# Three small moves in a written-out order of work: two jobs of the units 4n+2, the turning of the second batch's x, and a piece of context

## The chip, the cores and the metric

The kernel runs on one core of one Trainium2 chip. Its time is the device time of one execution in microseconds (us); lower is better. A profiled execution gives, for each engine, when each instruction ran. The engines are TensorE (PE, with its weight loads PEld), VectorE (DVE), ScalarE (ACT), GpSimd (POOL) and SyncE (SP), which here only issues transfers.

## The reference, cut to what matters

```python
B, LQ, D, LK = 4, 256, 512, 1601        # 32 query heads, 8 key heads of 128
q = layernorm(x) @ Wq + bq
k, v = split(ctx @ Wkv + bkv)
o = softmax(q @ k.T / sqrt(128)) @ v     # per batch and head; 4 query heads share k, v
x = x + tanh(g_xattn) * (o @ Wo + bo)
y = layernorm(x)
x = x + tanh(g_ffn) * (y @ base_W.T + top-2-of-8 LoRA experts of y)
```

All in float32. The matrix products of the attention are done as three products of rounded parts (high x high, high x low, low x high).

## The kernel before, in words

The attention is cut into 64 **units** U (4 batches of NU = 16), each with two query heads of one batch, 256 queries each, so 512 columns. A unit has 13 **slots** t, one for each tile of 128 context rows (the last has 65). Slot s = 13 U + t. In each slot PE does, first, three matmuls of scores into one of two psS buffers (L641), then three of probabilities x values for the tile of 19 slots before (L656 to L658), and then the **jobs** that a table gives to the slot (L663). The same table sets the order of work of all the other engines: each goes through the slots and waits on semaphores.

What follows a score tile: ACT copies it to xs (L917, called at L1018), DVE takes the running maximum into mrun (L1335), POOL subtracts the maximum (L846), ACT takes the exponential twice, as f32 (L1044) and rounded into ph (L1047), and DVE makes the low part pl (L1105) and the running sum psum_ (L1368). POOL does these two for one tile of a unit in the first batch, for three tiles in the others (L850, L855, L861). Scores of slot s may not start before the copy and the maximum of slot s - 2 are done (L638 to L640).

The jobs, by letter, with the unit n that they serve: m and s turn the running maximum and sum (n = U - 1, U - 2), b spreads the maximum over the lanes, q0 and q1 are the projections of the next unit's queries, k0 to k3 four pieces of Keys (k3 is 450 columns wide, the others 384), v0 to v12 pieces of Values, o0 and o1 the halves of the output projection of U - 2, p0 and p1 the same of U - 3, x0 and x1 turn the next batch's normalized x, r spreads the reciprocal sums by PE (in most units a transfer through memory does that instead, L984 to L995, and r is passed over; PE does it for the units n with n % 16 in (0, 12), so in the slots of U % 16 in (2, 14)).

The table has a row for each U % 4: AT in the first units, AT_MEM from U = 4 on, and TURN for the units 18, 34 and 50. The units 6, 10, 14, 22, 26, 30, 38, 42, 46, 54, 58 and 62 thus take the third row of AT_MEM, the row that the change edits.

Each job takes one of four banks of PSUM psW (`take`, L421). `free` is a queue in the order of issue: a job gets the bank that has been in the queue longest and waits for whoever empties it (`emptied`, L428): o and p halves are emptied by DVE's add into acc (L1144), k by DVE's kl (L1116), q by ql (L1128), s and m by reductions on DVE (L1266, L1244), b and r by ACT. From slot 6 on two banks hold attention outputs (pv), so two are left for the jobs.

The weights and the next batches' context are cut into high and low parts by POOL during the first batch (`cuts`, L837 and L839): the raw piece is fetched by SP to one of four staging buffers (`fetches`), and the parts go on to memory. The 16 pieces (c, n) of the second batch's context share one buffer cst, so each waits until the one before has been stored; x of the next batch is loaded to xraw and cst after the last of them (L774 to L778), normalized by POOL in slot 8 of unit 14, 30 or 46 (L896 to L900), and turned by PE in slots 11 and 12 of that unit.

In the loop of DVE, slot 26 (unit 2, t = 0) ends with the inverse standard deviation of six row tiles (L1393 to L1396).

Of the kernel before, what the change touches and what calls it, by code (L numbers as in the profile page):

```python
# [18 lines left out]
def gated_block(nc: bass.Bass, x, ctxT, gx, gf, wq, bq, wk, wv, bkv, wo, bo, bw, rw, la, lb,  # L19
# [12 lines left out]
    NU = 16  # L32
    UN = B * NU
# [16 lines left out]
    def lead(U):  # L50

        return 1 if U < NU else 3
# [3 lines left out]
    MEM_LO, MEM_SUM = 2, UN - 3  # L56

    def sum_by_mem(U):
        return MEM_LO <= U < MEM_SUM and U % NU not in (0, NU - 4)
# [9 lines left out]
    def on_slot(V):  # L69

        return 9 if sum_by_mem(V) else 8 if V < UN - 2 else 10 if V == UN - 2 else 6
# [3 lines left out]
    AT = [  # L75
# [4 lines left out]
    ]  # L80
    AT_MEM = [
# [4 lines left out]
    ]  # L86

    TURN = "m,v11 p0 b,v12 k2 p1 s k3 r q0 - q1 - o0"
    for U in range(UN + 2):

        names_of = {0: "k1 - k2 v0 q0 k3 q1 v1 - v2 - v3 -", UN: "- - - - - - - - s r - - o0",
                    UN + 1: "- p1 - - s c o0 o1",
                    UN - 1: "m - b - p1 s - r - - o0 - -"}.get(U, TURN if U > NU and U % NU == 2 else (AT_MEM if U >= MEM_LO + 2 else AT)[U % 4])
        for t, names in enumerate(names_of.split()):
            for name in names.split(","):
                kind, part = name[0], int(name[1:] or 0)
                n = {"m": U - 1, "b": U - 1, "s": U - 2, "r": U - 2, "o": U - 2, "p": U - 3, "q": U + 1, "v": U // 4,
                     "c": U - 2, "k": (U + 1) // 2, "x": U // NU + 1, "-": -1}[kind]
                top = {"m": UN, "b": UN, "s": UN, "r": UN, "o": UN, "c": UN, "p": UN - 1, "q": UN, "v": 4 * B, "k": NK, "x": B, "-": 0}[kind]
                if not 0 <= n < top or (kind == "x" and U % NU < 14):  # L100
                    continue
                if kind == "r" and sum_by_mem(n):
                    continue
                jobs[NT * U + t].append(("o" if kind == "p" else kind, n, part))
# [9 lines left out]
    def halves(kind, n):  # L114
        return [(kind, n, a) for a in range(2 if kind in "vo" else 1)]
# [7 lines left out]
    for U in range(NU + 1):  # L123
        at, u = NT * U, U % 4
        if U + 2 < NU:
            cuts[at + (9 if u == 2 else 7)] += halves("q", 2 * U + 4)
            cuts[at + (11 if u == 2 else 9 if u % 2 else 8)] += halves("q", 2 * U + 5)
        if u % 2 == 0 and U // 2 + 1 < 8:
            cuts[at + (8 if u == 2 else 9)] += halves("k", U // 2 + 1)
        if u == 3 and U // 4 + 1 < 4:  # L130
            for a in range(2):
                cuts[at + 9 + a].append(("v", U // 4 + 1, a))
        if U != 1:
            for a in range(2):
                cuts[at + (12 if U == 0 else 13 if u in (0, 3) else 18) + a].append(("o", max(U - 1, 0), a))
        for t in (9, 11) if u == 1 else (11,) if u != 3 or U == 3 else ():
            if spare:
                cuts[at + t].append(spare.pop(0))
    for n in range(16, 16 * (B - 1)):
        b, i = divmod(n, 16)  # L140
# [6 lines left out]
    stage, there, s = [], [[] for _ in range(4)], 0  # L147
    for no, (p, at) in enumerate(cut_at):
# [5 lines left out]
        if no >= len(first) + 2:  # L154
            s = max(s, at - 10, cut_at[last][1] + 1)
# [7 lines left out]
    with ExitStack() as ctx:  # L163
        def sb(name, shape, dt, c=ctx):
            return c.enter_context(nc.sbuf_tensor(name, shape, dt))
# [64 lines left out]
        x1 = sb("x1", [128, NQ - 2, 512], F32)  # L230
# [157 lines left out]
        for T in range(TN):  # L388
            U, t = divmod(T, NT)
# [705 lines left out]
        def _(eng):  # L1095
# [218 lines left out]
            def goes_first(kind, n, part):  # L1314

                return kind == "s" and sum_by_mem(n)

            def goes_later(kind, n, part):

                return kind == "yl" or kind == "o" and n == UN - 2  # L1320
# [16 lines left out]
            for s in range(SLOTS):  # L1337
                U, t = divmod(s, NT)
                b, u = divmod(U, NU)
                V = U - 2  # L1340
                for j in jobs.get(s - 1, []):
                    if goes_first(*j):
                        after_job(*j)
                if sum_by_mem(V):
                    divide(V, t - on_slot(V))
                if s < TN - 1:
                    running_max(s)
                if s == TN - 2:
                    running_max(TN - 1)
                    add_o(UN - 3, 0)  # L1350
                    row_max(UN - 1)
                if 0 <= V < UN and not sum_by_mem(V):
                    divide(V, t - on_slot(V))
                for j in jobs.get(s - 1, []):
                    if (j[0] not in "ms" or not TN - NT < s <= TN) and not goes_first(*j) and not goes_later(*j):
                        after_job(*j)
                T = s - EXP
                if 0 <= T < TN and T % NT >= lead(T // NT):
                    UT, tt = divmod(T, NT)
                    rows = rows_of(tt)  # L1360
                    p, total = exp_place(T), psum_[0:rows, UT % 2, :]
                    dve.wait_ge(s_h, T + 1)
                    lower(pl[0:rows, T % RP, :], p, ph[0:rows, T % RP, :]).then_inc(s_l)
                    if tt > lead(UT):
                        dve.wait_ge(s_a, a_count[T] - 1)
                    else:
                        dve.wait_ge(s_lp, lp_count[NT * UT])
                    eng.tensor_tensor(total, p, total, ALU.add).then_inc(s_a)  # L1368
                    if T == TN - 1:
                        total = psum_[:, UT % 2, :]  # L1370
                        dve.wait_ge(s_a, a_count[T])
                        dve.wait_ge(s_ap, 2 * (UT - NU) + 1)
                        eng.tensor_tensor(total, pair_of(UT)[:, 0, :], total, ALU.add).then_inc(s_a)
                for j in jobs.get(s - 2, []):
                    if goes_later(*j):
                        after_job(*j)
                if TN - NT <= s < TN:
                    for j in jobs[s]:
                        if j[0] in "ms" and not goes_first(*j) and j[1] != UN - 1:
                            after_job(*j)  # L1380
                if s in (0, 2):
                    lower_ctx(2 + s // 2)
                if s in (4, 13, 21):
                    r = (4, 13, 21).index(s) + 1
                    dve.wait_ge(s_acc, 16 * r)
                    for i in range(2):
                        stats(2 * r + i, acc[:, i, :])
                if s == 23:
                    floored_var(2, NQ)
                if s == 27:  # L1390
                    dve.wait_ge(s_bvh, 1)
                    lower(bvl[:, :], bkv_sb[:, 15:16], bvh[:, :]).then_inc(s_bvl)
                if s == 26:  # L1393
                    inverse_dev(2, 2, NQ)
                    eng.tensor_scalar(rstds[:, 2:NQ], rstd[:, 2:NQ], SCALE, None, ALU.mult).then_inc(s_stat)
                    dve.wait_ge(s_stat, 1)  # L1396
                if u == 2 and t == 6 and 1 <= b < B:
                    for i in range(2):
                        dve.wait_ge(s_acd, 32 * b)
                        stats(2 * b - 2 + i, acc[:, i, :])  # L1400
                if s == NT * (UN - 7) - 2:
                    floored_var(0, NQ - 2)
                if s == NT * (UN - 7):
                    inverse_dev(3, 0, NQ - 2)
                for i in {TN - 18: (0,), TN - 17: (1,), TN - 12: (3,), TN - 10: (5,)}.get(s, ()):
                    ffn_norm(i)
                if s == TN - 5:
                    dve.wait_ge(s_rtb, 1)
                    route_off(1)
                if s == TN - 3:  # L1410
                    route_first(1)
                if s == TN + 3:
                    route_second(1)
                if s == TN + 4:
                    route_weights(1)
# [84 lines left out]
```

## Time and profile before

| | |
|---|---|
| median of 3 runs | 2310.38 us (2306.56 to 2311.54) |
| the profiled execution's own time | 2311.37 us |
| its span | 2309.3 us |
| mean granted TensorE clock | 0.996 of full |
| instructions | 37402 |

The span is the time from the first to the last instruction of the profiled execution; its own time has some 2 us more. An engine's busy time is the time in which it ran instructions, and idle time is put down to the engine and line that it waited for.

### The profile page before, as it was taken

How to read it: one execution, taken by the hardware profiler on the slowest of the kernel's cores; microseconds unless marked ns; L12 is line 12 of the kernel's file. 1: busy time of each engine (PE TensorE's matmuls, PEld its weight loads, DVE VectorE, ACT ScalarE, POOL GpSimd, SP SyncE). 2: the span in 40 equal slices, each digit the busy share in tenths (PEclk: the TensorE clock that was granted, in tenths of full speed). 3: DMA queues.
4: the chain of work that ended last, by engine and by line, in shares of the span. 5: the costliest groups of instructions: out<-in, count | busy, mean ns of one | idle time of the engine just before them, and what ended most of it. 6: DMA issues, size and time to landing. Idle time of an engine off the chain costs nothing.

```text
span 2309.3 us, 37402 instructions
## 1 busy us (share of the span) xinstructions
PE 2262.2 (98%) x12363; PEld 1941.8 (84%) x12363; DVE 1815.1 (79%) x3167; ACT 1666.7 (72%) x3152; POOL 1633.0 (71%) x1372
## 2 busy tenths in 40 slices
PE   7999999999999999999999999999999999999998
PEld 6888888887888888888888888888888888888865
DVE  5888888887887787787778787787787778787786
ACT  4777777776777777777777777777777777777772
POOL 4888786977568678757658678776767756766772
PEclk9999999999999999999999999999999999999999
DMA  7344353564233242326213333333422213222111
GB/s 258 121 167 133 111 173 100 173 199 162 87 111 111 94 160 94 133 79 209 92 43 137 116 128 116 111 127 118 157 86 96 92 60 110 66 98 90 66 68 55
DMA packets 137567, 271.85 MB, mean 118 GB/s; under 512 B 21664, under 2 KB 54944, under 8 KB 137120
## 3 DMA queue, kind: packets, MB, share of 16 engines
q1 hardware_dynamic: 122400, 255.71, 32.6%
q10 hardware_dynamic: 14976, 13.74, 2.6%
q8 instruction: 101, 1.65, 0.3%
q14 instruction: 90, 0.74, 0.1%
HBM read 202.44 MB, written 66.97 MB: 117 GB/s over the span
## 4 chain that ended last, share of the span: by engine, by line
PE 79%; DVE 9%; POOL 5%; issue 3%; ACT 3%; DMA 1%; ACTq 0%; SPq 0%; POOLq 0%; DVEq 0%
PE psW L432 12%; PE psW L434 11%; PE psW L433 11%; PE psS L432 7%; PE psS L434 7%; PE psS L433 7%; PE psW L656 6%; PE psW L657 6%; PE psW L658 6%; POOL xs L846 3%; PE psW L488 3%; DVE psum_ L1368 3%; DVE mrun L1335 2%; PE psW L496 1%; DVE pl L1105 1%
## 5 line engine op out<-in xcount | busy, mean ns | idle before, releaser
L846 POOL TENSOR_TENSOR xs<-xs,mb 128x512 f32<-128x512 f32 (+1 forms) x832 | 1068.9, 1310 | 472.3 <-ACT mb L917 472.3
L1335 DVE TENSOR_TENSOR mrun<-psS,mrun 128x512 f32<-128x512 f32 (+1 forms) x704 | 482.8, 686 | 340.1 <-ACT xs L917 337.5
L917 ACT ACTIVATE xs<-psS 128x512 f32<-128x512 f32 (+1 forms) x832 | 496.0, 596 | 245.1 <-PE psS L434 232.4
L1105 DVE TENSOR_TENSOR pl<-psP,ph 128x512 fp32r<-128x512 f32 (+1 forms) x672 | 459.8, 684 | 81.5 <-ACT ph L1047 76.2
L1047 ACT ACTIVATE ph<-xs 128x512 fp32r<-128x512 f32 (+1 forms) x832 | 518.9, 624 | 3.3 <-PE psW L658 3.1
L1368 DVE TENSOR_TENSOR psum_<-psP,psum_ 128x512 f32<-128x512 f32 (+1 forms) x672 | 457.4, 681 | 1.0 <-POOL pl L850 0.9
L1044 ACT ACTIVATE psP<-xs 128x512 f32<-128x512 f32 (+1 forms) x672 | 401.2, 597 | 29.4 <-DVE rinv L1268 12.9
L432 PE MATMUL psS<-ql,kh 128*128 128x512 f32 (+1 forms) x832 | 340.3, 409 | 6.3 <-DVE mrun L1335 5.2
L656 PE MATMUL psW<-ph,vh 128*128 128x512 f32 (+1 forms) x832 | 335.4, 403 | 3.6 <-POOL pl L850 3.3
L433 PE MATMUL psS<-qh,kh 128*128 128x512 f32 (+1 forms) x832 | 328.8, 395 | 0.0
L434 PE MATMUL psS<-qh,kl 128*128 128x512 f32 (+1 forms) x832 | 328.7, 395 | 0.0
L657 PE MATMUL psW<-pl,vh 128*128 128x512 f32 (+1 forms) x832 | 328.3, 395 | 0.0
L658 PE MATMUL psW<-ph,vl 128*128 128x512 f32 (+1 forms) x832 | 328.2, 394 | 0.0
L432 PE MATMUL psW<-wvl,ch 128*128 128x256 f32 (+1 forms) x832 | 238.9, 287 | 0.0
L434 PE MATMUL psW<-wvh,cl 128*128 128x256 f32 (+1 forms) x832 | 233.9, 281 | 0.0
L433 PE MATMUL psW<-wvh,ch 128*128 128x256 f32 (+1 forms) x832 | 233.0, 280 | 0.0
L656 PEld LDWEIGHTS psW<-ph,vh 128*128 128x128 f32 (+1 forms) x832 | 156.5, 188 | 49.5 <-issue 7.2
L657 PEld LDWEIGHTS psW<-pl,vh 128*128 128x128 f32 (+1 forms) x832 | 157.2, 189 | 38.0 <-issue 2.4
L658 PEld LDWEIGHTS psW<-ph,vl 128*128 128x128 f32 (+1 forms) x832 | 156.6, 188 | 38.3
L434 PEld LDWEIGHTS psS<-qh,kl 128*128 128x128 f32 (+1 forms) x832 | 153.3, 184 | 39.4
L432 PE MATMUL psW<-cl,wkh 128*128 128x384 f32 (+1 forms) x512 | 178.8, 349 | 5.2 <-DVE cl L1105 5.2
L434 PE MATMUL psW<-ch,wkl 128*128 128x384 f32 (+1 forms) x512 | 178.9, 349 | 0.0
(208 smaller groups left out, 4382.8 us busy)
## 6 DMA issues: line engine op xcount, KB each, us to landing
wqh<-scr_wq SPq DMA_DIRECT2D x96, 256.0 KB, 2.6
wql<-scr_wq SPq DMA_DIRECT2D x96, 256.0 KB, 3.0
woh<-scr_wo SPq DMA_DIRECT2D x48, 512.0 KB, 3.3
wol<-scr_wo SPq DMA_DIRECT2D x48, 512.0 KB, 4.2
rbc<-scr_r ACTq DMA_DIRECT2D x52, 256.0 KB, 3.4
scr_wq<-wqh SPq DMA_DIRECT2D x32, 256.0 KB, 2.1
scr_wq<-wql SPq DMA_DIRECT2D x32, 256.0 KB, 2.5
scr_wo<-woh SPq DMA_DIRECT2D x16, 512.0 KB, 2.6
```

Source lines behind the costliest of these rows:

```text
L432: eng.matmul(o, lh, rl, start=first, stop=False)
L433: eng.matmul(o, lh, rh, start=False, stop=False)
L434: return eng.matmul(o, ll, rh, start=False, stop=last)
L656: eng.matmul(o, vh[0:rows, t, hs], hi, start=t == 0, stop=False)
L657: eng.matmul(o, vh[0:rows, t, hs], lo, start=False, stop=False)
L658: eng.matmul(o, vl[0:rows, t, hs], hi, start=False, stop=t == NT - 1).then_inc(s_pv)
L846: eng.tensor_tensor(tile, tile, mb[0:rows_of(t), U % 2, :], ALU.subtract).then_inc(s_sub)
L917: return eng.activation(hi, src, ACT.Copy)
L1047: eng.activation(ph[0:rows, T % RP, :], xs[0:rows, T % RX, :], ACT.Exp).then_inc(s_h)
L1105: return eng.tensor_tensor(lo, src, f32(hi), ALU.subtract)
L1335: eng.tensor_tensor(run, psS[0:rows, s % 2, :], a, ALU.max).then_inc(s_m)
L1368: eng.tensor_tensor(total, p, total, ALU.add).then_inc(s_a)
```

## The change

Five edits, all of order.

1. In the third row of AT_MEM, p0 goes from slot 4 to slot 1, k3 from slot 6 to slot 4, and in slot 7 the order of r and p1 is swapped.
2. For the second batch, x0 and x1 go from slots 11 and 12 of unit 14 to slots 1 and 2 of unit 15, where q0 goes from slot 1 to slot 7 (NEXT_X). Load and normalization of x stay where they are, and so do the turns of the third and fourth batch.
3. POOL cuts the context piece c3 in slot 26 instead of 37, and c4 in slot 37 instead of 50 (`(9, 11, 13) if U == 1`, and no `or U == 3`). Slot 50 loses its piece. The fetches move with them.
4. DVE's inverse standard deviation goes from slot 26 to slot 30 (unit 2, t = 4).
5. The condition on x names the three units.

```diff
@@ AT_MEM @@
-        "m,v11 - b,v12 k2 p0 s k3 r,p1 q0 - q1 x0 o0,x1",
+        "m,v11 p0 b,v12 k2 k3 s - p1,r q0 - q1 x0 o0,x1",
...
+    NEXT_X = "m x0 b,x1 k0 p1 s k1 q0 q1 k2 - o0 o1"
...
-                    UN - 1: "m - b - p1 s - r - - o0 - -"}.get(U, TURN if U > NU and U % NU == 2 else (AT_MEM if U >= MEM_LO + 2 else AT)[U % 4])
+                    NU - 1: NEXT_X, UN - 1: "m - b - p1 s - r - - o0 - -"}.get(U, TURN if U > NU and U % NU == 2 else (AT_MEM if U >= MEM_LO + 2 else AT)[U % 4])
...
-                if not 0 <= n < top or (kind == "x" and U % NU < 14):
+                if not 0 <= n < top or (kind == "x" and U not in (NU - 1, 2 * NU - 2, 3 * NU - 2)):
...
-        for t in (9, 11) if u == 1 else (11,) if u != 3 or U == 3 else ():
+        for t in (9, 11, 13) if U == 1 else (9, 11) if u == 1 else (11,) if u != 3 else ():
             if spare:
                 cuts[at + t].append(spare.pop(0))
...
-                if s == 26:
+                if s == 30:
                     inverse_dev(2, 2, NQ)
```

## Rows read from the trace of the kernel before

**Rows 1.** The page, busy us (share of the span) and instructions of each engine.

```profile
PE 2262.2 (98%) x12363; PEld 1941.8 (84%) x12363; DVE 1815.1 (79%) x3167; ACT 1666.7 (72%) x3152; POOL 1633.0 (71%) x1372
```

**Rows 2.** PE's waits: engine, line, waited for: us in total, times, longest.

```profile
PE psS L432 <- DVE mrun L1335: 5.2, 9, 0.7
...
PE psW L432 <- DVE kl L1116: 4.0, 5, 0.9
PE psW L656 <- POOL pl L850: 3.3, 3, 1.6
PE psW L488 <- POOL xraw L900: 2.8, 1, 2.8
```

**Rows 3.** Timeline, slots 11 and 12 of unit 14: start, us, instruction, [idle before].

```profile
537.02 0.39 PE L432 MATMUL psS<-ql,kh 128*128 128x512 f32 x1
...
541.41 0.65 PE L488 MATMUL psW<-ident,xraw 128*128 128x128 f32 x4 [2.83 <-POOL xraw L900]
...
546.62 0.48 PE L432 MATMUL psS<-ql,kh 128*128 128x512 f32 x1
```

**Rows 4.** A stretch of windows: busy of each engine, clock, DMA share, GB/s.

```profile
541.40:545.00 3.60, 3.59 (x12) 2.83 (x13) 1.27 (x3) 2.23 (x4) 3.60 (x3) 0.60 1.01 362
```

**Rows 5.** Timeline of POOL in unit 14, slots 8 to 12.

```profile
530.25 0.62 POOL L837 TENSOR_SCALAR woh<-pp 128x512 fp32r<-128x512 f32 x1 [7.93 <-PE psW L434]
...
541.34 2.08 POOL L900 TENSOR_SCALAR cst<-cst,mv,rstds 128x512 f32<-128x512 f32 x1
```

**Rows 6.** Timeline of PE in unit 30, from slot 7 to the start of unit 31.

```profile
1082.55 0.40 PE L432 MATMUL psS<-ql,kh 128*128 128x512 f32 x1
...
1086.90 0.39 PE L432 MATMUL psS<-ql,kh 128*128 128x512 f32 x1
...
1088.30 0.28 PE L432 MATMUL psW<-xtl,wqh 128*128 128x256 f32 x1
...
1093.93 0.39 PE L432 MATMUL psS<-ql,kh 128*128 128x512 f32 x1
...
1098.89 0.48 PE L432 MATMUL psS<-ql,kh 128*128 128x512 f32 x1
```

**Rows 7.** Timeline of DVE in unit 30, slot 8.

```profile
1088.43 0.69 DVE L1335 TENSOR_TENSOR mrun<-psS,mrun 128x512 f32<-128x512 f32 x1 [1.88 <-ACT xs L917]
...
1089.63 0.74 DVE L1144 SCALAR_TENSOR_TENSOR acc<-psW,tg,acc 128x512 f32<-128x512 f32 x1
```

**Rows 8.** Timeline of PE in unit 22: scores of slots 6 to 10 and 12.

```profile
803.45 0.47 PE L432 MATMUL psS<-ql,kh 128*128 128x512 f32 x1
807.39 0.40 PE L432 MATMUL psS<-ql,kh 128*128 128x512 f32 x1
810.15 0.39 PE L432 MATMUL psS<-ql,kh 128*128 128x512 f32 x1
812.97 0.39 PE L432 MATMUL psS<-ql,kh 128*128 128x512 f32 x1
814.36 0.40 PE L432 MATMUL psS<-ql,kh 128*128 128x512 f32 x1
...
819.31 0.42 PE L432 MATMUL psS<-ql,kh 128*65 128x512 f32 x1 [0.58 <-DVE mrun L1335]
```

**Rows 9.** Timeline of DVE in unit 22, slots 6 and 9.

```profile
805.18 0.18 DVE L1268 RECIPROCAL rinv<-ssum 128x4 f32<-128x4 f32 x1
...
814.13 0.69 DVE L1308 TENSOR_TENSOR psW<-psW,rbc 128x512 f32<-128x512 f32 x1
```

**Rows 10.** Timeline of DVE in unit 2, slots 1 and 5.

```profile
93.09 1.22 DVE L1162 TENSOR_TENSOR steps<-steps 128x6 f32<-128x6 f32 x1
...
107.15 0.69 DVE L1335 TENSOR_TENSOR mrun<-psS,mrun 128x512 f32<-128x512 f32 x1 [2.73 <-ACT xs L917]
```

**Rows 11.** Timeline of PE in unit 2, slot 2, and in unit 4, slot 6.

```profile
96.30 0.65 PE L496 MATMUL psW<-ident,nm 128*128 128x128 f32 x4 [1.21 <-DVE nm L1244]
...
172.81 0.47 PE L656 MATMUL psW<-ph,vh 128*128 128x512 f32 x1 [1.59 <-POOL pl L850]
```

## The prediction

> **What bounds the kernel now.** I read the page first: PE is busy for 2262.2 us, 98% of the span, the next engine for 79% [rows 1]. So time can only be won where PE stands still, 47 us in all, and the change adds and removes no matmul. Then PE's waits, which say for whom it stands [rows 2]: nine times for the running maximum (L1335, 0.7 at most), five times for a bank that kl empties (4.0 us), three times for POOL's pl (3.3), once for the normalized x (2.8). Then the timelines around those waits, and last the starts of the score matmuls, one for each slot, since the length of a slot shows a stall that is split over several instructions. In unit 22 a slot with no job takes 1.39 us (812.97 to 814.36), one with an output half 2.76 (slot 7), one with k3 3.94 (slot 6) [rows 8]. k3 so costs 3.94 - 1.39 = 2.55 (some 0.1 of it the slot's start behind a turn), a half 1.37. A move shifts PE's work, and what matters is how far DVE, ACT and POOL are behind PE afterwards.
>
> **Edit 2, x turned later.** In unit 14 PE stands 2.83 us before the first turn, for POOL's normalization [rows 3], and its clock then reads 0.60 over 3.6 us [rows 4], that is, most of them at 1.2 GHz. POOL is late because it stood 7.93 us for p1 in slot 7 and then worked without a break to 543.4 [rows 5]. Slots 11 and 12 together take 546.62 - 537.02 = 9.60 us [rows 3]; the same slots with the same jobs in unit 30 take 1098.89 - 1093.93 = 4.96 [rows 6]. The stall costs 4.64 us, its clock included. After the change the first turn is due some three slots later, at least 4.96 + 1.7 us after 537.0, and the normalized tiles are there at 541.4 and 543.4, so the whole 4.64 goes. The two turns cost the same in unit 15. There q0 comes in slot 7 where the slot had no job; DVE so gets a longer slot 7 and is less behind. For the small stalls of that unit that this closes I take an estimate of 0.5, within 0 to 1. Lower bound of the gain: the stall comes back at another place because POOL still has its 18 us to do; the places it could stop are the exponentials of the first slots of unit 15, which need POOL's subtraction: 1 us given back. Sum for this edit -5.1, from -3.6 to -5.6.
>
> **Edit 4, the inverse.** In unit 2 DVE's six small instructions run from 92.03 to 94.9, 2.9 us, ahead of the maximum and of the reduction for b, and PE waits 1.21 us for that [rows 11]; q0 in the next slot waits another 0.5 for DVE's kl, in the same backlog. At the new place, after the work of slot 30, DVE stood idle for 2.73 us waiting for a score copy [rows 10]. 2.9 in 2.73 leaves 0.2 to go through to r, which already waited. Sum -1.5, from 0 to -1.9. One instruction there took 1.22 us for six columns [rows 10], where the reciprocal of four columns took 0.18 [rows 9], so the 2.9 hold some 1.7 us that are not arithmetic. The Trainium skill (GPSIMD Engine Reference, section Specifications) says that GpSimd shares its SBUF interface with VectorE and contends with VectorE instructions that have two SBUF inputs. The trace agrees: 1.22 us is the time of a product of two SBUF tiles while POOL was at work. By the rule the 2.9 us stay 2.9 at the new place, where POOL is at work too; without it they could be some 1.2, and the 0.2 would be 0.
>
> **Edit 3, the context piece.** Before slot 6 of unit 4 PE waits 1.59 us for POOL's pl [rows 11], at the end of 40 us in which POOL never stood. The piece of slot 50 lies in that stretch and its two instructions took 0.52 and 1.02 us, so 1.5 us of the 1.59 go. In slot 26 the piece costs the same, but there POOL stands 3.4 us for unit 1's maximum; the bias additions of slot 28 are pushed to where that wait ends. SP waits at its fetch of c4 until c3 is stored, up to the end of unit 2's slot 3; behind it in the queue lie only fetches that are due ten slots later. If POOL is late there, the exponentials of unit 2 wait: at most 1.5 us. Sum -1.5, from 0 to -1.6.
>
> **Edit 1 in eight units without r (6, 10, 22, 26, 38, 42, 54, 58).** Here PE stands before slot 12 for the maximum of slot 10, 0.58 us in unit 22 [rows 8], and that is the last link of DVE's chain. I followed unit 22 with the clock at the start of slot 6 (803.45). Before: rinv at 1.73 [rows 9], slot 9 at 9.52, the first step of dividing (L1308) at 10.68 [rows 9], slot 12 at 15.86 [rows 8]. From the division to slot 12 it is 5.18 us, and that stays: division, oh and two exponentials on ACT, pl, sum, ol, maximum. After: slot 6 has no job. PE gets to slot 7 at 1.5, slot 8 at 4.25, slot 9 at 7.07: 2.45 us earlier than before. DVE and ACT cannot follow by so much. The sum's reduction, rinv and the copy that ACT issues behind it hold ACT till 3.4; from there, copy of slot 7, two exponentials, and then six DVE instructions of 0.6 us (pl, sum, maximum, the addition of p1, pl, sum) put the division at about 8.8, 1.9 us earlier. So slot 12 starts at 8.8 + 5.2 = 14.0, where PE alone would be there at 12.7: the wait grows from 0.75 us (slot length 2.14 against 1.39) to 1.3. A small wait in slot 2 goes (0.1), since p0 is between m and b. Per unit +0.4, six units +2.6. In units 6 and 10 DVE has two more pairs of pl and sum at just this place (the first batch), so +1.7 each; but PE's later arrival gives POOL the time for which the units behind, 7 and 11, wait at slot 6 (two of the three waits for pl in [rows 2]), and I take +0.4 for both. Sum +3.0; from -6 (all the waits of 0.75 us gone, 8 x 0.75) to +6 (nothing given back in units 7 and 11, and 0.4 more in each).
>
> **Edit 1 in four units with r (14, 30, 46, 62).** Now the slot 7 of unit 30 takes 4.35 us (1082.55 to 1086.90) [rows 6], against 1.39 + 1.37 + 0.35 for r = 3.11: a stall of 1.24, p1 waiting for the bank that kl of k3 empties (0.88 of it shown, four of the five waits in [rows 2]). It goes: k3 is two slots earlier. But the order of banks moves with it. With two banks from slot 6 on, the banks go s, p1, r, q0: before, q0 took the one of r, which ACT empties at once. Now p1 comes before r, and q0 takes p1's bank, which is free only after DVE's addition of p1. DVE does that behind the maximum of slot 8, and that needs slot 8's scores copied. In unit 30 the addition starts at 1089.63 and takes 0.74, so it ends 3.47 us behind the start of slot 8 [rows 6, 7], and that chain starts from PE itself, so it keeps its length. q0 started 1.40 behind it [rows 6]. The new stall is 3.55 - 1.45 = 2.1 us. Behind it DVE has caught up. Net +0.9 less the 0.1 in slot 2: +0.8 in three units. In unit 14 DVE has the first batch's two more pairs, the wait is 2.5 and the net +1.2. Sum +3.6, from +2 to +5. Behind q0 wait slot 9's scores only; SP's loads of the next q weights follow q0 by 2 us and have two slots to spare.
>
> **Sum.** -5.1 - 1.5 - 1.5 + 3.0 + 3.6 = -1.5 us. The clock comes on top. After 2.83 us of standing it fell, and cost some 1.6 of the 4.64 (slot 12 of unit 14, 4.80 us, against 3.2 in unit 30). After the 1.59 us in unit 4 it stayed. The four new waits of 2.1 to 2.5 us lie between; I take one fall of four, +1.6, and for the range none to four. That makes +0.1 on the profiled execution's own 2311.4 us, so 2311.5; that execution lies 1.0 above the median of three. Against the median 2310.4 it gives 2310.5, and as the unfollowed small waits around unit 15 and unit 2 are more likely to close than to open, I say 2310.
>
> **Rivals.**
> A. The waits before slot 12 close instead of growing, because k3's and the half's DVE work is gone from slots 7 and 8. For it: kl at slot 7 and its 0.6 us are in the chain now. Against it: PE gains 2.45 us on that chain and the chain 1.9. It gives -1.5 - 3.0 - 6 = -10.5 us, 2300. Chance 0.13.
> B. Clock falls. The place is q0 in slot 8 of units 14, 30, 46 and 62; the price 1.6 us a piece; it decides if a standstill of 2.1 us is enough. With four falls -1.5 + 6.4 = +4.9, 2315.3; with the upper ends of edit 1 beside it, 2320. Slower by over 0.2%. Chance 0.17.
> C. The turn's stall is only moved: POOL's queue of 18 us shows in unit 15. Then 3.6 to 4.6 us less are won, -1.5 + 4.6 = +3.1 at most, 2313. Chance 0.1; two slots of margin speak against it.
> D. q0's wait doesn't appear, as DVE reaches the addition sooner than from the copy of slot 8. Against it: the order in the loop is written out, the maximum first. The new stalls (3.6) are then missing and the old ones (4 x 1.24) gone: -1.5 - 3.6 - 5.0 = -10.1, 2300. Chance 0.08.
> My forecast, gains and losses that cancel within 4 us: 0.52.
>
> Faster or slower by over 0.2% (4.6 us) is about what a measurement of this kernel can tell from no change. Faster: A, D and the lower tail of the forecast (0.06), 0.27. Slower: B's greater part (0.12) and a fifth of C: 0.14. Within: 0.59. Range 2301 to 2317: it holds A's near half and B with part of its upper ends.
>
> **What the profile would show.** Unit 14's slots 11 and 12 under 5 us together, no 1.2 GHz there. A PE wait of 2.1 us at the first wqh matmul of slot 8 in units 14, 30, 46, 62, on DVE acc L1144, in place of that on kl. Slot 11 of unit 22 at 2.7 us against 2.14. No wait for nm in unit 2, none above 0.2 for pl in unit 4. The prediction is wrong if slot 11 in unit 22 shrinks towards 1.4, or if slot 8 in unit 30 stays at 2.8.

## The result: slower by 0.5%

The changed kernel takes 2319.84 us in the median of 4 runs (2319.41 to 2320.86), the kernel before 2308.47 us in the runs beside it (2305.9 to 2311.54). The ratio is 1.0050, 95% interval 1.0038 to 1.0062. The forecast was 2310 and its range ended at 2317. The measured time lies above both: the kernel got slower where no change was expected. The profiled execution's own time is 2320.86 us, its span 2319.0, which is 9.7 more than before. (Lines of the changed kernel stand two higher: L1335 is now L1337.)

**After, the page.** The head of the page, and the busy time of each engine.

```profile
span 2319.0 us, 37387 instructions
...
PE 2267.6 (98%) x12363; PEld 1943.9 (84%) x12363; DVE 1817.6 (78%) x3167; ACT 1667.0 (72%) x3152; POOL 1630.4 (70%) x1372
```

Beside [rows 1] no engine has more work worth the name. PE's 5.4 us are the same matmuls, some of them at the lower clock.

**After, PE's waits.** Who ended them; us in total, times, longest.

```profile
PE psS L434 <- DVE mrun L1337: 10.3, 9, 2.6
...
PE psW L434 <- DVE acc L1146: 8.5, 4, 2.4
```

Beside [rows 2] the waits for kl (4.0) and for the normalized x (2.8) are gone from the head of the list, and no wait for POOL's pl is left in it. In their place stand 8.5 us on acc, four times, which the forecast had (8.8), and 5.1 more on the running maximum, one of them 2.6 long, which it had not.

**After, timeline of PE**, where the new stops and the starts of slots lie: unit 2 slot 7; unit 6 slots 11 and 12; unit 14 slots 8 and 11 and the start of unit 15; unit 22 slots 11 and 12; unit 30 slot 8.

```profile
107.11 0.47 PE L434 MATMUL psS<-ql,kh 128*128 128x512 f32 x1 [2.63 <-DVE mrun L1337]
...
258.78 0.50 PE L658 MATMUL psW<-ph,vh 128*128 128x512 f32 x1 [0.61 <-DVE pl L1107]
260.72 0.41 PE L434 MATMUL psS<-ql,kh 128*65 128x512 f32 x1 [0.98 <-DVE mrun L1337]
...
536.12 0.35 PE L434 MATMUL psW<-xtl,wqh 128*128 128x256 f32 x1 [2.37 <-DVE acc L1146]
...
541.83 0.39 PE L434 MATMUL psS<-ql,kh 128*128 128x512 f32 x1
...
545.99 0.39 PE L434 MATMUL psS<-ql,kh 128*128 128x512 f32 x1
...
816.91 0.39 PE L434 MATMUL psS<-ql,kh 128*128 128x512 f32 x1
819.32 0.42 PE L434 MATMUL psS<-ql,kh 128*65 128x512 f32 x1 [0.85 <-DVE mrun L1337]
...
1089.82 0.35 PE L434 MATMUL psW<-xtl,wqh 128*128 128x256 f32 x1 [2.06 <-DVE acc L1146]
```

Read against [rows 3], slots 11 and 12 of unit 14 take 545.99 - 541.83 = 4.16 us where they took 9.60: edit 2 does what it should. Read against [rows 8], slot 11 of unit 22 takes 2.41 where it took 2.14.

**After, timeline of DVE in unit 2**, the inverse in its new slot 30:

```profile
99.77 0.18 DVE L1162 RECIPROCAL rstd<-steps 128x6 f32<-128x6 f32 x1
99.98 1.29 DVE L1163 TENSOR_TENSOR steps<-rstd 128x6 f32<-128x6 f32 x1
101.30 1.22 DVE L1164 TENSOR_TENSOR steps<-steps 128x6 f32<-128x6 f32 x1
102.56 1.22 DVE L1165 TENSOR_SCALAR steps<-steps 128x6 f32<-128x6 f32 x1
103.82 1.20 DVE L1166 TENSOR_TENSOR rstd<-rstd,steps 128x6 f32<-128x6 f32 x1
105.05 1.20 DVE L1397 TENSOR_SCALAR rstds<-rstd 128x6 f32<-128x6 f32 x1
106.28 0.69 DVE L1337 TENSOR_TENSOR mrun<-psS,mrun 128x512 f32<-128x512 f32 x1
```

**After, timeline of POOL** over the same time:

```profile
97.44 2.54 POOL L848 TENSOR_TENSOR xs<-xs,mb 128x512 f32<-128x512 f32 x2
99.94 1.31 POOL L852 TENSOR_TENSOR pl<-psum_,ph 128x512 fp32r<-128x512 f32 x1
101.21 6.23 POOL L848 TENSOR_TENSOR xs<-xs,mb 128x512 f32<-128x512 f32 x5
```

The six instructions take 6.5 us, not 2.9, and then the maximum runs for which PE stands. Five of them work on six columns and take 1.2 us each; the reciprocal, on as many columns, takes 0.18. POOL starts an instruction at 101.21 and then about every 1.25 us (102.46, 103.70, 104.95, 106.17). The five DVE instructions end at 101.27, 102.53, 103.78, 105.01 and 106.24, each 0.06 to 0.08 us behind one of these starts. So it is one DVE instruction for each POOL instruction.

**After, clock in two stretches.** PE busy with its count, the granted clock, DMA share, GB/s:

```profile
108.00:114.50 6.50, 6.05 (x18) 0.50 0.54 184
...
1090.90:1094.30 3.40, 3.40 (x12) 0.51 0.34 91
```

Both are at 1.2 GHz, right behind a standstill (2.63 and 2.06 us).

**Where the 9.7 us are**, by the starts of the units' first slots, after less before: unit 2 +3.3; unit 4 -1.6; units 6 to 12 +4.2; unit 14 -4.1 and unit 15 +0.3; units 22, 26, 38, 42, 54, 58 +3.7; units 30, 46, 62 +5.9; unit 63 +0.8; all others together some -0.4; and -2.4 up to the end of unit 0, which no edit touches. There the profile before happens to have 1.2 GHz (granted clock 0.50) from 23.3 to 26.7 and from 30.2 to 37.0 us, where that of the changed kernel reads 1.00. The four other profiles of this study with two such stretches are within 0.2 us of the kernel before; the nine with less or none of it are 2.0 to 3.3 us shorter. So two single profiles can differ by 2 or 3 us where no edit is at work, and the units have to be compared one by one.

### The profile page after: what moved, and what is told of

Same layout as the page of the kernel before. It is cut to its first block, busy times and chain, and to the rows that moved or that the text cites. A ratio compares the mean times of both kernels' runs of the same rounds, so it can differ in the third digit from the quotient of the medians.

```text
span 2319.0 us, 37387 instructions
## 1 busy us (share of the span) xinstructions
PE 2267.6 (98%) x12363; PEld 1943.9 (84%) x12363; DVE 1817.6 (78%) x3167; ACT 1667.0 (72%) x3152; POOL 1630.4 (70%) x1372
## 4 chain that ended last, share of the span: by engine, by line
PE 83%; DVE 8%; issue 3%; ACT 3%; POOL 1%; DMA 1%; ACTq 0%; SPq 0%; DVEq 0%
PE psW L434 12%; PE psW L436 12%; PE psW L435 12%; PE psS L434 7%; PE psS L436 7%; PE psS L435 7%; PE psW L658 7%; PE psW L660 7%; PE psW L659 7%; PE psW L490 3%; DVE psum_ L1370 2%; DVE mrun L1337 2%; PE psW L498 1%; ACT ph L1049 1%; DVE pl L1107 1%
## 5 line engine op out<-in xcount | busy, mean ns | idle before, releaser
L1337 DVE TENSOR_TENSOR mrun<-psS,mrun 128x512 f32<-128x512 f32 (+1 forms) x704 | 481.9, 684 | 347.4 <-ACT xs L919 346.4
L434 PEld LDWEIGHTS psS<-ql,kh 128*128 128x128 f32 (+1 forms) x832 | 154.9, 186 | 28.5 <-ACT xs L919 11.3
```

The source lines that it names most:

```text
L434: eng.matmul(o, lh, rl, start=first, stop=False)
L1337: eng.tensor_tensor(run, psS[0:rows, s % 2, :], a, ALU.max).then_inc(s_m)
```

## The experiments

All are timed beside the kernel before, which took 2307.3 to 2309.0 us in the four sets. An expectation stands ahead of each result as it was put down before the run.

**1. The inverse back.** The changed kernel with edit 4 undone.

```diff
-                if s == 30:
+                if s == 26:
```

> The changed kernel with DVE's inverse deviation back in slot 26; all other edits stay. Theory P (port): at slot 30 five of its small instructions take 1.2 to 1.3 us each beside POOL's subtractions (0.8 and 1.2 us for two of them at slot 26), which stops PE for 2.6 us before slot 7 of unit 2 and then lowers its clock; so unit 2 gives back 4.5 to 5.5 us and the kernel is 2315 us. Rival C (the context piece): the wait in unit 2 comes from POOL being later by the piece in slot 26; then unit 2 still stands 2 to 3 us in slot 6 or 7 and the time is 2319 or 2320.

2317.23 us (2313.38 to 2318.25), 1.0036 (1.0024 to 1.0047). Unit 2 is 2.18 us shorter than before, and the stop before slot 7 is gone. Timeline of DVE, and below it of POOL, at the old place:

```profile
89.11 0.18 DVE L1162 RECIPROCAL rstd<-steps 128x6 f32<-128x6 f32 x1
89.33 0.17 DVE L1163 TENSOR_TENSOR steps<-rstd 128x6 f32<-128x6 f32 x1
...
90.13 0.17 DVE L1397 TENSOR_SCALAR rstds<-rstd 128x6 f32<-128x6 f32 x1
```

```profile
87.41 1.31 POOL L848 TENSOR_TENSOR xs<-xs,mb 65x512 f32<-65x512 f32 x1
90.64 0.51 POOL L839 TENSOR_SCALAR cst<-stg 128x384 fp32r<-128x384 f32 x1 [1.92 <-DMA scr_c<-pp]
```

POOL stands from 88.7 to 90.64 and each DVE instruction takes 0.17. So edit 4 costs 5.4 us of unit 2 in the profile, as expected. The time fell by 2.6 us between the medians (3.2 between the ratios, whose intervals allow 5.4), to 2317 and not to 2315; the spans of the two profiles differ by 3.6, since small waits and stretches at 1.2 GHz lie at other places too. Rival C is out. Further, the waits of slots 2 and 3 that edit 4 was to win go without it: with the context piece of edit 3 in slot 26, POOL stands for a store there, and the inverse runs in that pause.

**2. The inverse alone.** The kernel before with edit 4.

```diff
-                if s == 26:
+                if s == 30:
```

> The kernel before with the inverse deviation in slot 30 and nothing else. Theory P: unit 2 is longer by 3 to 5 us (a stop of about 2.6 us before slot 7, the clock at 1.2 GHz behind it, less the 1.2 + 0.5 us of waits in slots 2 and 3 that go): 2311 to 2313 us. Rival C: without the piece in slot 26 the stop is not there and the kernel is 1.5 to 2 us faster than before, 2307.

2311.75 us (2308.77 to 2313.61), 1.0013 (1.0004 to 1.0021). Unit 2 is 3.24 us longer: slots 2 and 3 give 2.19, slots 6 to 8 take 5.74. The five small instructions take 1.19 to 1.23 us here too. No context piece was moved, so it is not the piece: the stop before slot 7 (2.53 us) comes with the inverse alone.

**3. r ahead of p1.** The changed kernel with the old order in slot 7.

```diff
-        "m,v11 p0 b,v12 k2 k3 s - p1,r q0 - q1 x0 o0,x1",
+        "m,v11 p0 b,v12 k2 k3 s - r,p1 q0 - q1 x0 o0,x1",
```

> The changed kernel with the old order r, p1 in slot 7 of the row; k3 and p0 stay in slots 4 and 1. Theory B (banks): q0 in slot 8 of units 14, 30, 46 and 62 gets the bank of r, which ACT empties, in place of p1's, so the four stops of 2.0 to 2.4 us on the addition go, with the clock falls behind two of them: 10 to 12 us less in those slots. Something may come back in slots 9 to 12 as PE runs ahead of DVE: up to 1 us a unit. 2309 to 2312 us. Rival: the stop is DVE's backlog and not the bank; then PE stops as long in slot 9 or 10 and the time stays within 2 us of 2320.

2319.49 us (2314.02 to 2322.26), 1.0044 (1.0032 to 1.0057). The four stops at q0 are gone, and units 30 and 46 are each 0.9 us shorter than before: the bank was the reason. But the expected 2309 to 2312 was missed, and the number is the rival's. In this profile four other places are worse than in that of the changed kernel: unit 0 by 2.6 us (the two stretches at 1.2 GHz again), slot 6 of unit 2 by 5.2, slot 2 of unit 15 by 2.1, slot 10 of unit 62 by 2.4. The profiled execution, 2321.88 us, is among the slowest of six that spread over 8 us, so it is not shown that the others lost at the same places. Timeline of DVE in unit 2 and in unit 62:

```profile
102.50 8.31 DVE L1163 TENSOR_TENSOR steps<-rstd 128x6 f32<-128x6 f32 x1
...
2201.39 4.09 DVE L1181 TENSOR_SCALAR hn<-x,mv,rstd 128x512 f32<-128x512 f32 x1
```

A product of six columns took 8.31 us, over eight instructions that POOL ran in a row (101.5 to 110.8). It waits for POOL as the five of the changed kernel do, but for several instructions at a time.

**4. The later x and the context pieces alone.** The kernel before with edits 2, 3 and 5.

```diff
+    NEXT_X = "m x0 b,x1 k0 p1 s k1 q0 q1 k2 - o0 o1"
...
-        for t in (9, 11) if u == 1 else (11,) if u != 3 or U == 3 else ():
+        for t in (9, 11, 13) if U == 1 else (9, 11) if u == 1 else (11,) if u != 3 else ():
```

> The kernel before with the two edits that only moved waits of POOL: x turned in unit 15, and c3 and c4 cut earlier; the row and the inverse as before. By the unit lengths of the changed kernel: units 14 and 15 are 5 us shorter, unit 4 1.6 us shorter, nothing lost elsewhere: 2302 us, 0.3 % faster. Rival: the gains of unit 14 depend on the row's edit (k3 earlier), and only 2 to 3 us are won: 2305 us.

2303.53 us (2299.09 to 2304.76), 0.9975 (0.9966 to 0.9984): these two pay. Unit 2 -2.2, unit 4 -1.5, unit 14 -5.4, but unit 15 +2.4, so the later x alone wins 3.0 us in the two units and not the 5 that were expected. Timeline of PE in unit 15, slots 2 and 3, and of POOL ahead of it:

```profile
540.68 0.48 PE L434 MATMUL psS<-ql,kh 128*128 128x512 f32 x1
...
542.61 0.50 PE L658 MATMUL psW<-ph,vh 128*128 128x512 f32 x1 [0.98 <-DVE pl L1107]
...
544.40 0.65 PE L498 MATMUL psW<-ident,nm 128*128 128x128 f32 x4 [0.82 <-DVE nm L1246]
...
545.25 0.48 PE L434 MATMUL psS<-ql,kh 128*128 128x512 f32 x1
```

```profile
526.18 0.62 POOL L839 TENSOR_SCALAR woh<-pp 128x512 fp32r<-128x512 f32 x1 [7.92 <-PE psW L436]
...
535.21 2.11 POOL L902 TENSOR_SCALAR xraw<-xraw,mv,rstds 128x512 f32<-128x512 f32 x1
537.28 2.10 POOL L902 TENSOR_SCALAR cst<-cst,mv,rstds 128x512 f32<-128x512 f32 x1
539.32 5.05 POOL L848 TENSOR_TENSOR xs<-xs,mb 128x512 f32<-128x512 f32 x4
```

This is rival C at half its price: POOL's two normalizations stand ahead of the subtractions that unit 15 needs. In the changed kernel it hardly shows (slots 2 and 3 of unit 15 +1.0), since the stop at q0 in slot 8 of unit 14 has already made PE late; in experiment 3, without that stop, slot 2 of unit 15 takes 4.53 us as it does here (4.56), against 2.47 in the changed kernel.

**5. The row alone.** The kernel before with edit 1.

```diff
-        "m,v11 - b,v12 k2 p0 s k3 r,p1 q0 - q1 x0 o0,x1",
+        "m,v11 p0 b,v12 k2 k3 s - p1,r q0 - q1 x0 o0,x1",
```

> The kernel before with the new row of slots alone (edit 1: k3, p0, p1 and the output half in their new slots), all else as before. Theory R (the row is what costs, by three mechanisms that the profile after shows: the wait of q0 in slot 8 of the four units with r for the bank of p1, 2.0 to 2.4 us each; a wait before slot 12 of the other eight units that is some 0.4 us longer each; and a clock fall here and there behind them): units 30, 46, 62 together +4 to +6 us, the six units from 22 on together +3.7, units 6 to 12 +4, so 2317 to 2319 against a before of 2308.5. Rival (the row itself cost near nothing, and what unit 30 and the others lose comes with the later x or the inverse): 2308 to 2311.

2321.15 us (2317.81 to 2324.7), 1.0059 (1.0045 to 1.0072), more than the 2317 to 2319 that I had put on it. The rival is out. By units: 6 to 12 +4.8; 22, 26, 38, 42, 54, 58 +4.4; 30, 46, 62 +5.9; 14 -1.7; 63 +0.9. Its waits of PE:

```profile
PE psW L432 <- DVE acc L1144: 8.5, 4, 2.4
PE psS L432 <- DVE mrun L1335: 7.9, 8, 1.0
...
PE psW L656 <- DVE pl L1105: 3.7, 9, 0.6
```

The factors of experiments 5, 4 and 2 multiply to the result: 1.0059 x 0.9975 x 1.0013 = 1.0047, against 1.0050 measured. So, within the intervals, the row is all of the loss; the others nearly cancel, to -0.12%.

**6. The good half of the row.** The kernel before with a row of its own in units 14, 30, 46 and 62.

```diff
+    TURN_R = "m,v11 p0 b,v12 k2 k3 s - r,p1 q0 - q1 x0 o0,x1"
...
-                    UN - 1: "m - b - p1 s - r - - o0 - -"}.get(U, TURN if U > NU and U % NU == 2 else (AT_MEM if U >= MEM_LO + 2 else AT)[U % 4])
+                    UN - 1: "m - b - p1 s - r - - o0 - -"}.get(U, TURN_R if U > 4 and U % NU == 14 else TURN if U > NU and U % NU == 2 else (AT_MEM if U >= MEM_LO + 2 else AT)[U % 4])
```

> The kernel before with a row of its own in the four units with r (14, 30, 46, 62): k3 two slots sooner, p0 in slot 1, and r ahead of p1, so that q0 takes the bank that ACT empties; the eight other units keep the old row. Theory (the wait of p1 for the bank that kl of k3 empties goes, 1.24 us each, and no wait of 2 us takes its place): about 0.9 us less in each of units 30, 46 and 62, unit 14 the same or less, 2305 to 2306. Rival (the stop only moves on: POOL or DVE are late somewhere in the next slots, as in slot 10 of unit 62 with this order in the changed kernel): 2308 to 2310.

2306.8 us (11 runs, 2304.5 to 2308.76), 0.9994 (0.9985 to 1.0003). By units 14 -0.5, 30 and 46 -0.9 each, 62 -0.3. That is the forecast mechanism except in unit 62, at a time 0.8 us above the expected one, and too little to be told from no change by the time alone.

**7. The inverse where POOL stands.** The changed kernel with it in slot 83.

```diff
-                if s == 30:
+                if s == 83:
```

> The changed kernel with the inverse of the columns' deviations in slot 83 (unit 6), where POOL stands for the maximum, in place of slot 30. Theory P (each small DVE instruction waits for the POOL product that is running, so the price is set by whether POOL is at work and not by the columns): the six instructions take 1.1 to 1.6 us together there, no stop before slot 7 of unit 2, unit 2 shorter than before by 2.2 us, 2314.5 to 2317. Rival (they take about 1.2 us each wherever they stand): 6.5 us in unit 6, and 2319.

2316.59 us (2312.75 to 2317.65), 1.0037 (1.0024 to 1.0049). Timeline of DVE there:

```profile
242.27 0.17 DVE L1163 TENSOR_TENSOR steps<-rstd 128x6 f32<-128x6 f32 x1
242.47 0.17 DVE L1164 TENSOR_TENSOR steps<-steps 128x6 f32<-128x6 f32 x1
242.67 0.17 DVE L1165 TENSOR_SCALAR steps<-steps 128x6 f32<-128x6 f32 x1
242.87 0.17 DVE L1166 TENSOR_TENSOR rstd<-rstd,steps 128x6 f32<-128x6 f32 x1
243.07 0.17 DVE L1397 TENSOR_SCALAR rstds<-rstd 128x6 f32<-128x6 f32 x1
```

Timeline of POOL:

```profile
244.41 0.62 POOL L839 TENSOR_SCALAR woh<-pp 128x512 fp32r<-128x512 f32 x1 [4.96 <-PE psW L436]
```

POOL stands from 239.4 to 244.4, and the same five instructions take 0.85 us in place of 6.1, as expected; the rival is out. Unit 2 is 5.5 us shorter than in the changed kernel.

**8. What pays, together.** The kernel before with edits 2, 3 and 5, the row of experiment 6, and the inverse in slot 83.

```diff
+    NEXT_X = "m x0 b,x1 k0 p1 s k1 q0 q1 k2 - o0 o1"
+    TURN_R = "m,v11 p0 b,v12 k2 k3 s - r,p1 q0 - q1 x0 o0,x1"
...
-                if s == 26:
+                if s == 83:
```

> The kernel before with the later x, the moved context pieces, the inverse in slot 83, and the row of the four units with r changed as in the run beside this one; the eight other units keep the old row. Theory: the two edits that pay (2303.5 with them alone) and 0.9 us in each of three units, 2300 to 2302. Rival (with the later x, POOL is the bound in units 15, 31 and 47 and eats what is won in slot 8 before them): 2303 to 2305.

2302.11 us (2298.37 to 2304.32), 0.9976 (0.9966 to 0.9986), just above the expected range and not to be told from experiment 4, so that neither theory nor rival is shown by the time. Units 14, 30, 46 and 62 are 2.5 us shorter than there; unit 6, where the inverse now stands, is 1.2 longer (slots 8 and 11), and unit 15 1.3 longer, with 1.2 GHz from 542.8 to 546.2 us behind its stops in slot 2.

**9 to 11. POOL's normalizations sooner.** In experiment 9 on top of experiment 4, in 10 on the kernel before, in 11 on experiment 4 with the row of experiment 6.

```diff
-                if u == 14 and t == 8 and b + 1 < B:
+                if u == 14 and t == 4 and b + 1 < B:
```

> The kernel before with the later x and the moved context pieces (2303.5 so), and POOL's two normalizations for the next batch issued four slots sooner, in slot 4 of unit 14, ahead of the piece of wo for whose staging POOL stands 7.9 us. Theory (what PE loses in slot 2 of unit 15 is POOL's 4.2 us of normalization ahead of the subtractions that the first slots of unit 15 need): the stops of 0.97 and 0.81 us in slot 2 of unit 15 go, unit 15 shorter by some 2.4 us, 2301. Rival (the stops come from DVE's and ACT's work on the turned tiles in the same slots): unit 15 as it was, 2303.5.

> The kernel before with nothing but POOL's two normalizations issued four slots sooner; x is turned in unit 14, slots 11 and 12, as before. Theory (the stop of 2.83 us there is POOL being late and nothing else): the stop and the clock fall behind it go, slots 11 and 12 of unit 14 together about 5 us, 2304 to 2305 against 2308.5; the later turn is then not needed. Rival (slots 11 and 12 are held by ACT's and DVE's work on the turned tiles too): 2306 to 2308.

> The kernel before with the later x, the moved context pieces, the early normalizations and the new row of the four units with r (k3 two slots sooner, p0 in slot 1, r ahead of p1), the inverse in its old slot 26. Theory: unit 2 -2.2, unit 4 -1.5, unit 14 -5.4, unit 15 0, units 14, 30, 46 and 62 another -0.3, -0.9, -0.9, -0.3 against before: 2308.5 - 11.5 on the profile, 2298 to 2300. Rival (gains of under 1 us in a stop are given back later): 2301 to 2303.

9: 2310.59 us, 1.0008 (0.9999 to 1.0017). 10: 2314.73 us, 1.0024 (1.0015 to 1.0033). 11: 2307.15 us, 0.9988 (0.9979 to 0.9998). All three expectations were missed, and all at places that I had not looked at. The theory itself held: slot 2 of unit 15 gave back 2.06 us in 9, slots 11 and 12 of unit 14 gave 4.63 in 10. But the line is in a loop over three batches, and in the queue of POOL it now stood ahead of pl. Timeline of PE in unit 30, slot 6, and of POOL, in experiment 9:

```profile
1072.47 0.79 PE L658 MATMUL psW<-ph,vh 128*128 128x512 f32 x1 [2.93 <-POOL pl L852]
```

```profile
1067.05 2.08 POOL L902 TENSOR_SCALAR xraw<-xraw,mv,rstds 128x512 f32<-128x512 f32 x1
1069.12 2.08 POOL L902 TENSOR_SCALAR cst<-cst,mv,rstds 128x512 f32<-128x512 f32 x1
1071.16 1.26 POOL L852 TENSOR_TENSOR pl<-psum_,ph 128x512 fp32r<-128x512 f32 x1
```

In 9, unit 30 lost 5.8 us (6.8 us of it at 1.2 GHz, around the stop), unit 46 3.2, unit 14 1.7; in 10, units 30 and 46 lost 5.9 and 3.2. In 11 units 30 and 46 were 1.9 us longer than before where 0.9 less was expected, and unit 62 was 2.5 longer; there hn, a normalization of 128 rows by DVE, took 4.12 us.

**12. The normalizations in POOL's standstill.** As 11, but in slot 5 and behind that slot's pl, in unit 14 alone; and the row of experiment 6 in units 14, 30 and 46 alone.

```diff
+                b, left = divmod(s, NT * NU)
+                if left == NT * 14 + (8 if b else 5) and b + 1 < B:
+                    pool.wait_ge(s_stat, 1)
...
                 for p in cuts[s]:
                     cut(*p)
...
-                if u == 14 and t == 4 and b + 1 < B:
```

> The kernel before with the later x, the moved context pieces, the new order (k3 two slots sooner, p0 in slot 1, r ahead of p1) in units 14, 30 and 46 alone, and POOL's two normalizations of unit 14 issued in slot 5, behind the slot's pl and ahead of the piece of wo for whose bank POOL stands 7.9 us; in units 30 and 46 they stay in slot 8. Theory (POOL has 4.2 us to spare in that standstill and nowhere else in unit 14; the losses of the early normalizations were all pl standing behind them): unit 2 -2.2, unit 4 -1.5, unit 14 -5.8, unit 15 about 0, units 30 and 46 -0.9 each against before, 2298 to 2300. Rival (the normalizations in the standstill still hold something up, or unit 15's stops come from DVE): 2301 to 2304.

2298.75 us (2296.84 to 2301.34), 0.9953 (0.9939 to 0.9967): 0.5% faster than the kernel before, as much as the change under study is slower. Unit 2 -2.2, unit 4 -1.6, unit 14 -5.8, unit 15 +0.3, units 30 and 46 -0.9 each; unit 63, which no edit touches, +1.5 (slots 10 and 11 at 1.2 GHz). The expectation held. Timeline of POOL:

```profile
519.79 2.08 POOL L889 TENSOR_SCALAR xraw<-xraw,mv,rstds 128x512 f32<-128x512 f32 x1
521.87 2.07 POOL L889 TENSOR_SCALAR cst<-cst,mv,rstds 128x512 f32<-128x512 f32 x1
526.08 0.62 POOL L841 TENSOR_SCALAR woh<-pp 128x512 fp32r<-128x512 f32 x1 [2.14 <-PE psW L438]
```

The 4.2 us lie in what was a standstill of 7.9 [rows 5], and POOL still stands for 2.14 behind them.

## Why the prediction was wrong, step by step

**Edit 2, the later x: the number right, partly by luck.** -5.1 forecast; unit 14's two slots -5.4 and unit 15 +0.3, -5.1. The stall in unit 14 went as forecast. But alone the edit wins 3.0 us, because POOL's two normalizations then stop PE in slot 2 of unit 15 (experiments 3 and 4). In the changed kernel the new stop at q0 hides that; the prediction had added the two edits as if they did not touch each other.

**Edit 3, the context piece: right.** -1.5 forecast, -1.6 measured in unit 4. Its larger effect was not seen: the pause that it gives POOL in slot 26 is what empties slots 2 and 3 of unit 2 (-2.2, experiments 1 and 4).

**Edit 4, the inverse: the step that failed in kind.** The prediction read a duration of 2.9 us off the old place [rows 10] and laid it into 2.73 us of idle time. The row of 1.22 us for six columns was seen there, and the sentence that "By the rule the 2.9 us stay 2.9 at the new place" drew the wrong conclusion from it. At the old place POOL was at work only while the first two of the five ran; the rest took 0.17. The price is per instruction: five times what POOL's instruction leaves, 6.1 us beside the reciprocal's 0.2, in 2.73 us of room; the stop of 2.63 follows, and 1.2 GHz behind it. +3.3 in unit 2 against -1.5. Experiment 2 shows it for this edit alone, experiments 1 and 7 that the price goes where POOL stands. The -1.5 was for waits in slots 2 and 3; they did go (2.2 us), but with edit 3 they go without it (experiments 1 and 4).

The trace agrees with what the Trainium skill (SBUF — State Buffer, section Who interferes with whom) states: a VectorE instruction with two SBUF inputs contends with a GpSimd instruction that reads SBUF, and one in a two-port mode, which tensor_scalar can enter, contends with GpSimd; the one issued first holds the shared ports for its whole length and the other blocks. Here it is 1.2 us behind a POOL instruction of 1.25, for the products and the tensor_scalars, and 0.17 to 0.18 when POOL stands or, beside POOL, for the reciprocal. DVE's large instructions that read PSUM and SBUF keep their 0.68.

**Edit 1, eight units without r: a mis-sized term.** Forecast +2.6 for six units, measured +3.7, and in experiment 5 +4.4; the mechanism is the forecast one (0.58 before slot 12 became 0.85 to 0.99, with a wait for DVE's pl beside it in units 38 and 54). No run takes the moves of p0 and k3 apart, so which of the two costs this stays open. For units 6 and 10 with what stands behind them the forecast was +0.4, measured +4.2. The +1.7 each were there and more (unit 10 +1.7; unit 6 +3.6, of which 1.6 is slot 12 at 1.2 GHz). What I set against them was 3.0 us of waits in units 7 and 11; slot 6 there gave back 1.00 and 1.23 but slot 11 took 0.88 and 0.57, so 0.7 us was won in place of 3.0. This is the largest miss within edit 1. Rival A is out: no wait before slot 12 closed.

**Edit 1, four units with r: right, and the clock a little more.** The stops are 2.37, 2.06, 2.05 and 2.05 us against 2.5 and 2.1 forecast, on acc, in slot 8; experiment 3 shows that the bank is the cause. Rival D is out. The falls behind these stops were two, where one was taken. Unit 30, with one, lost 2.7; unit 46, without, 1.2; the difference of 1.6 is the price that was taken from before. Together, with unit 14's share (+1.4), +7.3 against 5.2.

**The sum.** By the times of the whole kernel: the row costs 13.6 us (0.59%) where 8.2 was forecast, one clock fall included; the inverse costs 3.0 where it was to win 1.5; edits 2 and 3 win 5.8 where 6.6 was forecast. Together that is +10.8 against +0.1, and the changed kernel is 11.4 slower.

By the units of the two profiles: forecast +0.1. What was missed: unit 2 4.8, the eight units 4.9, the four units 2.1, unit 63 0.8, together 12.6; less 2.4 at the start, 0.1 of edit 3 and some 0.4 in all other units. That makes 9.8, and the spans differ by 9.7. Cut the other way, the clock is a large part of it: slots 7 and 8 of unit 2 (2.9 us longer), slot 12 of unit 6 (1.6) and units 30 and 62 (1.6 each) are 7.7 us lost at 1.2 GHz, where the forecast had 1.6. So rival B had the right sign and a part of the reason, but of its four falls at q0 two came, and the dearest one stood behind a stop that the forecast did not have. The range ended at 2317 because the upper ends were not added up: -3.6 + 0 + 0 + 6 + 5 and four falls are +13.8, 2324. And the inverse had no end on the side of a loss.

**Left open.** What decides whether the clock falls behind a standstill of about 2 us: of the 16 stops at q0 in the changed kernel and in experiments 1, 5 and 7 eight were followed by 1.2 GHz, and the same stop was followed by it in one kernel and not in another. Unit 63 is a second case of the same: in slot 10 PE stands for 1.41 to 1.44 us in all 14 profiles; in eight of them the clock is at 1.2 GHz from there on and slots 10 and 11 take 1.5 to 1.6 us more, in the other six it is not. So the 0.8 us of unit 63 are not the change's.

## What to carry to other kernels

A duration read off a trace belongs to its neighbours: before a short VectorE instruction is moved, look what GpSimd does at the new place, and price it at one GpSimd instruction at least, or put it where GpSimd stands. When a job is moved in a queue of banks, write down who empties the bank that the next job now takes; swapping two jobs in one slot cost 1.7 and 2.1 us in units 14 and 46 here, and 3.6 in unit 30, where the clock fell behind the stop (the changed kernel against experiment 3; the time of the whole kernel did not show it). When one issue is moved to an engine's pause, move it behind what is due in that slot, and in the iteration in question alone. And two edits whose waits lie on the same engine a few slots apart are not to be added up: one can hide what the other costs.

## What was unexpected of the hardware

How long VectorE is kept out is not bounded by one GpSimd instruction. The normalization hn (TENSOR_SCALAR, 128x512, in unit 62) is the same in all 14 kernels of this study and meets POOL's subtractions of 1.3 us in each. In three profiles it took 0.53 or 0.54 us and ended 0.3 us behind the start of a subtraction that came out 1.5 us long. In six it took 0.87 to 0.93 and ended 0.3 us behind a subtraction with which POOL's row ended, so it had no gap to take. In two it took 1.60: one subtraction, and then it got in between two. In the other three it took 4.09, 4.12 and 4.31: it let three gaps pass and ended 0.3 us behind the last of five subtractions (6.3 us) that POOL ran in a row. Six columns took 2.62 us in experiment 10 and 8.31 in experiment 3. So VectorE got in between two instructions of GpSimd in five of the eight profiles where hn met an unbroken row, and in the other three missed every gap. That makes the price of one such instruction anything from nothing to the length of GpSimd's run of work, and why it gets in or not stays open.
